# A macaron layer on one core: a new beginning, the value product split in the last blocks, and another order of the work after attention

## The reference, cut to what matters

```python
x = x + 0.5 * ffn(layernorm(x), W_r, W_k, W_v, mu_r, mu_k)
x = x + attn(layernorm(x), Wq, Wk, Wv, Wu, Wo)
x = x + 0.5 * ffn(layernorm(x), W_r, W_k, W_v, mu_r, mu_k)

# ffn:  x_prev is x one token earlier (zero for the first)
xr = mu_r * x + (1 - mu_r) * x_prev ;  xk = mu_k * x + (1 - mu_k) * x_prev
out = sigmoid(xr @ W_r.T) * (square(relu(xk @ W_k.T)) @ W_v.T)
# attn: 16 heads of 16; q, k, v, u are projections, kv = k.T @ v over all tokens of a sequence
out = (srms_norm(relu(q) @ kv) * silu(u)) @ Wo.T
```

## Time and profile before

| | |
|---|---|
| median of 3 runs | 323.25 us |
| profiled execution | 323.19 us |
| its span (first to last instruction) | 321.5 us |
| TensorE busy | 309.6 us, 96% |
| TensorE weight loads busy | 280.2 us, 87% |
| VectorE busy | 239.8 us, 75% |
| ScalarE busy | 239.7 us, 75% |
| GpSimd busy | 215.0 us, 67% |

### The profile page before, as it was taken

One profiled execution on the slowest core, in us unless ns is written; L12 is line 12 of the kernel. 1 busy time (PEld: TensorE's weight loads), 2 busy tenths in 40 slices (PEclk: granted clock), 3 DMA queues, 4 the chain that ended last, 5 costly groups with the idle time before them and its releaser, 6 DMA issues.

```text
span 321.5 us, 5807 instructions
## 1 busy us (share of the span) xinstructions
PE 309.6 (96%) x2052; PEld 280.2 (87%) x2052; DVE 239.8 (75%) x566; ACT 239.7 (75%) x465; POOL 215.0 (67%) x234
## 2 busy tenths in 40 slices
PE   6898999999999999999999999999999999998996
PEld 6677898899889988988988998889998989887985
DVE  3689984595675746895894797686989988995744
ACT  3698967969869679679259367479797979679861
POOL 4297858769778578669358217536687979797560
PEclk9999999999999999999999999999999999999999
DMA  7960000000000000000000000000002020121103
GB/s 215 352 219 0 3 1 0 2 0 2 0 1 3 0 2 0 0 2 0 2 2 0 2 0 2 0 3 1 2 1 67 0 67 0 66 67 66 65 2 131
DMA packets 11036, 10.85 MB, mean 34 GB/s; under 512 B 768, under 2 KB 11008, under 8 KB 11008
## 3 DMA queue, kind: packets, MB, share of 16 engines
q1 hardware_dynamic: 10432, 10.23, 9.8%
q10 hardware_dynamic: 576, 0.26, 0.3%
HBM read 6.29 MB, written 4.19 MB: 33 GB/s over the span
## 4 chain that ended last, share of the span: by engine, by line
PE 68%; DVE 15%; POOL 7%; issue 5%; ACT 4%; DMA 1%; SPq 0%; POOLq 0%; ACTq 0%
PE psK L1077 7%; PE psK L1078 7%; PE psK L1079 7%; PE psRV L1077 6%; PE psRV L1079 6%; PE psRV L1078 6%; PE psX L1078 6%; PE psX L1077 6%; PE psX L1079 6%; PE psK L1234 2%; PE psA L1094 2%; PE psX L1161 2%; PE psRV L1146 2%; DVE head_ss L892 1%; POOL gout L265 1%
## 5 line engine op out<-in xcount | busy, mean ns | idle before, releaser
L806 DVE SCALAR_TENSOR_TENSOR mix<-psA,mu,mix 128x512 f32<-128x512 f32 x64 | 44.0, 741 | 11.1 <-ACT mix L525 11.1
L359 POOL TENSOR_TENSOR mix_k_lo<-mix,mix_k_hi 128x512 fp32r<-128x512 f32 x30 | 39.2, 1328 | 12.9 <-ACT mix_k_hi L543 12.8
L525 ACT ACTIVATE mix<-psA,one_mu 128x511 f32<-128x511 f32 x64 | 39.5, 696 | 2.2 <-PE psA L1094 2.2
L512 ACT ACTIVATE xn<-xs,shiftA,rstdA 128x256 f32<-128x256 f32 x59 | 30.8, 603 | 12.4 <-POOL shiftA L343 12.4
L1077 PE MATMUL psRV<-ffn_hi,mix_r_hi 128*128 128x256 f32 x128 | 36.4, 284 | 0.0
L1079 PE MATMUL psRV<-ffn_hi,mix_r_lo 128*128 128x256 f32 x128 | 35.8, 279 | 0.0
L1078 PE MATMUL psRV<-ffn_lo,mix_r_hi 128*128 128x256 f32 x128 | 35.7, 279 | 0.0
L1077 PE MATMUL psK<-mix_k_hi,ffn_hi 128*128 128x512 f32 x64 | 26.1, 408 | 1.8 <-DVE mix_k_lo L961 1.5
L1077 PE MATMUL psRV<-ffn_hi,act_hi 128*128 128x256 f32 x96 | 27.5, 287 | 0.0
L1079 PE MATMUL psRV<-ffn_hi,act_lo 128*128 128x256 f32 x96 | 26.8, 279 | 0.0
L1078 PE MATMUL psRV<-ffn_lo,act_hi 128*128 128x256 f32 x96 | 26.8, 279 | 0.0
(11 more groups left out here) (157 smaller groups left out, 1066.3 us busy)
## 6 DMA issues: line engine op xcount, KB each, us to landing
xs<-x_dram SPq DMA_DIRECT2D x7, 512.0 KB, 8.7
out_dram<-xs SPq DMA_DIRECT2D x7, 512.0 KB, 2.9
out_dram<-xs SPq DMA_DIRECT2D x4, 128.0 KB, 1.7
xs<-x_dram ACTq DMA_DIRECT2D x2, 128.0 KB, 2.9
xs<-x_dram SPq DMA_DIRECT2D x2, 128.0 KB, 2.6
silu_u<-w_ffn_k_dram SPq DMA_DIRECT2D x1, 256.0 KB, 5.0
q_store<-w_k_dram SPq DMA_DIRECT2D x1, 256.0 KB, 5.2
silu_u<-w_ffn_r_dram SPq DMA_DIRECT2D x1, 256.0 KB, 6.5
```

What stands on the lines that cost most here:

```text
L359: nc.gpsimd.tensor_tensor(mix_k_lo[:, h, :], mix[:, 0, h, :], mix_k_hi[:, h, :].bitcast(F32), ALU.subtract).then_inc(s_lo_k, 1)
L512: nc.scalar.activation(xn[:, t, :], tile_row(xs, b, t), ACT.Identity, bias=shiftA[:, t:t + 1], scale=rstdA[:, t:t + 1]).then_inc(s_xn, 1)
L525: nc.scalar.activation(mix[:, rk, h, 1:BLOCK], psA[:, h, 0:BLOCK - 1], ACT.Copy, scale=one_mu[:, rk, h:h + 1]).then_inc(s_prev, 1)
L806: nc.vector.scalar_tensor_tensor(out=m, in0=psA[:, h, :], scalar=mu[:, rk, h:h + 1], in1=m, op0=ALU.mult, op1=ALU.add).then_inc(s_mix, 1)
```

## The change

- **Beginning.** mu_k and mu_r come in as two rows of 1 KB each (`mu_rows`), TensorE turns them with two small transposes into psK, VectorE copies them to `mu` and only then normalizes tiles 0 to 2 of block 0. K(0) is plain fp32: no high or low part of mix, and raw W_k. Idle transposes: 24, the two of mu, 6, then A(0), none after. TensorE goes A(0), means of k and u, K(0), A(1), R(0), mean of q, V(0), a wait for W_k's low part, K(1), A(2), B(0), R(1), ... The mean of v moves into i = 3, into psA, and its centring behind `r_low(4)`. The weights' DMAs go ffn_k, x1, ffn_r, k, u, ffn_v, q, v. VectorE normalizes all of block 1 and half of block 2; low parts move between GpSimd and VectorE.
- **V.** Passes 13, 14 and 15 are split; only 12 stays plain. ScalarE makes relu and the rounded square; VectorE makes the exact square in psK, in place (`act_low2`), and subtracts. V(15) writes psA and psK.
- **Orders.** K(14) and K(15) run their products with c outside; K(13), K(14) come ahead of A(14), A(15). `add_attention` moves ahead of `stats_b` in i = 6 and 7; GpSimd's `x1_low(7)` goes ahead of `norm_second(2)` and `scales_a(9)` behind `kt_low(7)`; VectorE's `stats_a(9)` goes behind `mix_current(8)`. Passes 12 to 15 are written out on each engine.
- `SPLIT_O` and `g_t` go; j < 8 always held, so `project_out` and `keep_g_rows` issue what they did.

The core of the diff:

```diff
-        xn_vector = {0: (0, 1, 2), LAST: (2, 3)}
+        xn_vector = {0: (0, 1, 2), 1: (0, 1, 2, 3), 2: (0, 1)}
...
             scales_a(0)
-            pool.wait_ge(s_ffn_hi, 1)
             pool.wait_ge(*normalized(0, 2))
-            nc.gpsimd.tensor_tensor(ffn_lo[:, 0, :, :], raw_of(0), ffn_hi[:, 0, :, :].bitcast(F32),
-                                    ALU.subtract).then_inc(s_ffn_lo[0], 1)
+            for i in (0, 1):
+                pool.wait_ge(s_ffn_hi, i + 1)
+                nc.gpsimd.tensor_tensor(ffn_lo[:, i, :, :], raw_of(i), ffn_hi[:, i, :, :].bitcast(F32),
+                                        ALU.subtract).then_inc(s_ffn_lo[i], 1)
             scales_a(1)
-            r_low(0)
-            act_squares(0)
+            act_low(0)
+            k_low(1)
             scales_a(2)
-            k_low(1)
+            pool.wait_ge(*normalized(2, 1))
             weights_low((0, 1, 2))
...
+            norm_second(7)
+            scales_a(14)
+            add_ffn2(11)
+            k_low(13)
+            r_low(13)
+            scales_a(15)
+            add_ffn2(12)
+            k_low(14)
+            r_low(14)
+            add_ffn2(13)
+            k_low(15)
...
+            def act_low2(n):
+                for h in range(HALVES):
+
+                    dve.wait_ge(s_act_hi, lows(n - 1) + h + 1)
+                    nc.vector.scalar_tensor_tensor(out=psK[:, h, :], in0=psK[:, h, :], scalar=0.0, in1=act_k[:, h, :],
+                                                   op0=ALU.max, op1=ALU.mult).then_inc(s_act, 1)
+
+                    dve.wait_ge(s_act, 2 * (n - NB) + h + 1)
+                    nc.vector.tensor_tensor(act_lo[:, h, :], psK[:, h, :], act_hi[:, h, :].bitcast(F32),
+                                            ALU.subtract).then_inc(s_act_lo, 1)
...
             stats_a(0)
+            dve.wait_ge(s_mu_t, 1)
+            nc.vector.tensor_copy(mu[:].rearrange("p r h -> p h r"),
+                                  psK[:, 0, 0:2 * HALVES].rearrange("p (h r) -> p h r", r=2)).then_inc(s_mu, 1)
+            dve.wait_ge(s_mu, 1)
+            nc.vector.tensor_scalar(one_mu[:], mu[:], -1.0, 1.0, ALU.mult, ALU.add).then_inc(s_one_mu, 1)
             normalize_some(0)
...
+            stats_a(1)
+            for rk in range(2):
+                for h in range(HALVES):
+                    mix_one(0, rk, h)
             next_column(0)
-            ffn_weight_low(1)
-            center_weight("k", 1)
+            normalize_some(1)
+            r_low(0)
+            center_weight("k", 2)
+            center_weight("u", 2)
+            ffn_weight_low(2)
+            mix_current(1)
+            center_weight("q", 3)
             stats_a(2)
...
+            r_low(1)
             gate_ffn(0, 0)
+            normalize_some(2)
             add_ffn1(0, 0)
...
+            act_low2(13)
+            mix_current(14)
+            gate_ffn(13, 0)
+            gate_ffn(13, 1)
+            act_low2(14)
+            mix_current(15)
             gate_ffn(14, 0)
             gate_ffn(14, 1)
+            r_low(15)
+            act_low2(15)
...
+                if n == 0:
+
+                    pe.wait_ge(s_w_in["ffn_k"], 16)
+                    for m in range(HALVES):
+                        for c in range(HALVES):
+                            if m == 0:
+                                pe.wait_ge(s_mix, mix_part(0, 0, c))
+                            last = nc.tensor.matmul(psK[:, m, :], raw_ffn[:, 0, c, tok(m)], mix[:, 0, c, :],
+                                                    start=(c == 0), stop=(c == HALVES - 1))
+                        last.then_inc(s_k, 1)
...
-            keep_clock_up(40)
+            keep_clock_up(24)
+            pe.wait_ge(s_mu_in, 32)
+            for h in range(HALVES):
+                last = nc.tensor.transpose(psK[:, 0, 2 * h:2 * h + 2],
+                                           mu_rows[:].rearrange("r (p h) -> r h p", h=HALVES)[:, h, :], ident[0:2, 0:2])
+            last.then_inc(s_mu_t, 1)
+            keep_clock_up(6)
             transpose_a(0)
-            keep_clock_up(4)
             weight_mean("k")
-            pe.wait_ge(s_ffn_lo[0], 1)
+            weight_mean("u")
             ffn_k(0)
-            weight_mean("u")
-            weight_mean("q")
             transpose_a(1)
             pe.wait_ge(s_ffn_lo[1], 1)
             ffn_r(0)
-            weight_mean("v")
+            weight_mean("q")
             pe.wait_ge(s_ffn_lo[2], 1)
             ffn_v(0)
...
+            ffn_k(13, [(s_relu, 26)])
+            transpose_a(14)
+            ffn_r(13)
+            ffn_v(13)
+            ffn_k(14, [(s_act_lo, lows(13))])
+            transpose_a(15)
+            ffn_r(14)
+            ffn_v(14)
+            ffn_k(15, [(s_act_lo, lows(14))])
             ffn_r(15)
+            ffn_v(15)
```

More of the change, by code:

```diff
@@ L32 @@
 HELD = 5
-SPLIT_O = 8
 FFN_W = ("ffn_k", "ffn_r", "ffn_v")
@@ L508, in normalize @@
                     act.wait_ge(s_tA, 2 * n)
-                for t in range(TILES):
+                for t in tiles:
                     if t in xn_vector.get(n, ()):
@@ L721, in _ @@
             normalize(9)
-            for n in range(8, 13):
+            for n in range(8, 12):
                 j = n - 5
@@ L937, in finish_last @@
                     gated = gate_of(LAST)[:, t // 2, cols]
-                    nc.vector.scalar_tensor_tensor(out=gated, in0=(psRV, psX)[t % 2][:, t // 2, 0:D], scalar=0.5,
+                    nc.vector.scalar_tensor_tensor(out=gated, in0=last_of(t), scalar=0.5,
                                                    in1=gated, op0=ALU.mult, op1=ALU.mult).then_inc(s_gated_last, 1)
@@ L1009, in _ @@
                 add_ffn1(i, 1)
+                if i == 6:
+                    add_attention(0)
                 stats_b(i)
                 r_low(i + 1)
+                if i == 3:
+                    center_weight("v", 4)
                 keep_g(i - 1)
@@ L1015, in _ @@
                 if i == 6:
-                    add_attention(0)
                     stats_a(8)
@@ L1027, in _ @@
                 add_ffn1(7, g)
+            add_attention(1)
             stats_b(7)
-            add_attention(1)
             gate_heads(2)
@@ L1032, in _ @@
             x2_low(7)
-            stats_a(9)
             keep_g(6)
             mix_current(8)
+            stats_a(9)
             projections(7)
@@ L1038, in _ @@
             gate_heads(3)
-            r_low(8)
             add_attention(2)
             keep_g(7)
+            r_low(8)
             stats_a(10)
             mask_kv(1)
-            for n in range(8, 13):
+            for n in range(8, 12):
                 j = n - 5
@@ L1056, in _ @@
                 mix_current(n + 1, (1,))
-                if j + 1 < NB:
-                    gate_heads(j + 1)
-            for n in range(13, LAST):
-                gate_ffn(n - 1, 0)
-                gate_ffn(n - 1, 1)
-                if n == 13:
-                    add_attention(NB - 1)
-                    stats_a(LAST)
-                mix_current(n + 1)
-                if n + 2 <= LAST:
-                    normalize_some(n + 2)
-                r_low(n + 1)
+                gate_heads(j + 1)
+            gate_ffn(11, 0)
+            gate_ffn(11, 1)
+            add_attention(6)
+            head_norms(7)
+            stats_a(14)
+            mix_current(13, (0,))
+            g_low(7)
+            mix_current(13, (1,))
+            gate_ffn(12, 0)
+            gate_ffn(12, 1)
+            add_attention(7)
+            stats_a(15)
+            act_low2(13)
[4 more added lines that the diff above has]
+            mix_current(15)
             gate_ffn(14, 0)
             gate_ffn(14, 1)
+            r_low(15)
+            act_low2(15)
+            for g in range(2):
+                dve.wait_ge(s_gate, 2 * LAST + g + 1)
             finish_last()
@@ L1259, in project_out @@
                     for c in range(HALVES):
-                        if j < SPLIT_O:
-                            last = product(dst, g_hi[:, c, tok(t)], g_lo[:, c, tok(t)], wo_hi[:, c, :],
-                                           wo_lo[:, c, :], c == 0, c == HALVES - 1)
-                        else:
-                            last = nc.tensor.matmul(dst, g_t[:, c, tok(t)], wo[:, c, :],
-                                                    start=(c == 0), stop=(c == HALVES - 1))
+                        last = product(dst, g_hi[:, c, tok(t)], g_lo[:, c, tok(t)], wo_hi[:, c, :],
+                                       wo_lo[:, c, :], c == 0, c == HALVES - 1)
                     if t % 2:
```

267 lines of the change are left out of this document (131 added, 136 removed).

## The result

The changed kernel takes 317.64 us (median of 6 runs, 317.39 to 317.80), the kernel before 323.18 in the same session (322.29 to 323.69): a ratio of 0.983, 95% interval 0.9817 to 0.9844. The forecast was 319.9, range 318.2 to 322.6.

A forecast was written before the change was run, and what follows sets the result against it. TensorE's work, the beginning and the end were taken to bound the kernel. Head -2.2, v's mean +0.85, `gram(7)` -0.9 and V(13) to V(15) -1.1 gave -3.35 on 323.19: 319.84, as median 319.9 us, range 318.2 to 322.6.

The forecast's parts named there:

- First us: Beginning up to A(0): mu's transposes end near 7.8, VectorE normalizes from 8.4, 1.7 us late, costing nearly nothing.
- K(0): In the head: plain K(0) starts at 12.1 against 13.14, takes 3.3 us, ends at 15.4, 1.0 earlier.
- To R(1): Head from A(1) on: earlier VectorE chain, both adds at 1.05; R(1) 2.2 us earlier, bounds 0 to 3.3.
- Mean of v: Moved into a stretch where TensorE has no idle time: costs 0.85 us.
- `gram(7)`: Its second half no longer waits for k_lo, as mix(8) comes earlier: -0.9 us, between 0 and -1.0.
- V(13) to V(15): End of kernel: splitting saves 0.44 each for 13 and 14; first gate 1.1 us earlier, bounds +1.4 to -1.8.
- Rival (b): Passes 13 to 15: VectorE's square in PSUM is slow, 1.4; +2.5 on the end, 322.4 us; chance 0.08.
- rival (a): Head given back: adds beside att_lo, or ScalarE's load, hold B(0) or KU(0); head 0.5, 321.6 us; chance 0.20.
- rival (c): Beginning: TensorE starts again at half pace, A(0) through A(1) up to twice as long; +5.9, 325.8 us; chance 0.06.
- Rival (d): More than forecast: the waits of R(0) and in passes 14 and 15 go; 318.3 us; chance 0.11.

The follow-up runs named there:

- the busy GpSimd: Changed kernel plus one extra 128x512 GpSimd product, released by the third tile of block 1's xn; 318.86 us, ratio 0.9867.
- the cold start: Changed kernel with 4 idle transposes in place of 24 and none behind mu's; 318.15 us, ratio 0.985.

## Why the prediction was wrong, by its own steps

**First us: right in time, wrong in price.** mu's transposes were forecast to end near 7.8 (VectorE's copy started at 7.83), xn from 8.4 (8.11). "Costs nearly nothing" was wrong: mu as columns is 0.8 earlier at R(1). The step looked at A(0) behind the idle transposes and not at VectorE's chain, which starts at xn and sets nearly everything up to R(1).

**K(0): right.** Start 12.1 forecast, 11.87 measured; 3.3 taken, 3.43 measured; end 15.4, measured 15.30. The trade it described is shown by the split K(0).

**To R(1): this step failed.** It gave 2.2 and measured 3.87. The term is mis-sized by 1.67, most of the miss of 2.25; even the latest of the eleven traces with this beginning (R(1) at 29.78) leaves 1.1 of it. In pieces, along VectorE's list:

- xn of block 1 ended at 14.9, not 15.6. 0.3 of this is the earlier start at 8.11; for the rest the forecast gives no steps to compare.
- r's low part was charged 1.9, its second half stretched by GpSimd, and took 1.29 for two, unstretched. R(0) began at 16.27, not 17.5.
- mix of block 1 ended at 21.2, not 22.6: ScalarE's `previous(1)`, forecast to be the late part there, was in time, and VectorE never waited. The first gate ended at 25.2, not 26.8.
- The first add was charged 1.05 and took 0.69. But VectorE waited 0.30 ahead of it for block 2's 1/sqrt, which the forecast did not have: GpSimd's two instructions for it took 0.53 and 1.24 beside VectorE's low part of r, where such instructions take 0.19 and 1.02 alone. The second add, stretched as forecast, ended at 28.57, not 30.3.

So the mechanism that failed is the contention: it was charged to VectorE at each meeting with GpSimd, and never to GpSimd. The earlier trace rows showed an add of 0.70 and one of 1.05, but not who came first. GpSimd's row of the trace of before has it, the product at 30.49 ahead of the add at 31.38:

```profile
30.49 3.08 POOL L387 TENSOR_TENSOR att_lo<-q_store,att_hi 128x512 fp32r<-128x512 f32 x2 [1.49 <-ACT att_hi L501]
```

The changed kernel and the busy GpSimd show the rule: the engine that comes second waits. The Trainium skill, SBUF — State Buffer, section "SBUF: two separate sides", has just this for a VectorE instruction with two SBUF inputs: whichever of it and GpSimd's instruction starts first holds the shared ports for its whole instruction, and the other blocks. The traces agree, with 1.29 against 2.21 on VectorE and 2.34 on GpSimd. A small slip beside it: the 30.9 given for B(0) is R(1)'s start, 0.69 behind the last add as in the trace of before.

**Mean of v: right**, 0.85 forecast, 0.65 measured over i = 3. **`gram(7)`: right**, 0.9 forecast, 1.0 measured, and the order put back costs 1.3.

**V(13) to V(15): the size nearly right, the reason wrong, so partly luck.** The first gate came 27.54 after O(7)'s end (27.65 forecast, 28.8 before), and V(13) waits for nothing. But the 0.44 for each split V is not there: plain V is as fast. What left is the wait for the sigmoid of pass 13 (1.07), through the new orders. The forecast had ScalarE's order in its timeline, but gave it no price of its own. The finish was called bound by VectorE at 0.87 per tile; at that pace it was bound by plain V(15) on TensorE. With the split V it went to 0.80 (310.49 to 312.88 for three tiles), now VectorE's own pace, a gain of 0.2. That 0.2 does not show in the median against plain V(15), whose first gate comes earlier. No run has the new orders alone in the old end, so that they are enough by themselves is argued, not shown.

Rival (b) is refuted by 0.70 for the instruction from PSUM to PSUM, rival (a) by R(1), rival (c) by the 1.83 and 3.43 of the changed kernel's means and K(0), and in its price by the cold start. Rival (d), 318.3, had the right direction for a reason half right: R(0)'s wait did go, those of passes 14 and 15 partly stayed.
